# Two self-attention stages with their q·k products in float32 on 32-row head tiles instead of bfloat16 parts in one long stack

## The reference

```python
Q, K, V = (split_heads(x @ W.T) for W in (Wq, Wk, Wv))      # layer 0; 16 heads of 16
scores  = einsum('bhqd,bhkd->bhqk', Q, K) / 4 + mask        # mask: 0 where q-64 <= k <= q, else -1e9
x       = x + (softmax(scores) @ V merged) @ Wo.T           # on a normalised x

q, k, v = (split_heads(x @ W + b) for each of q, k, v)      # layer 1
x       = x + (softmax(q k^T / 4) @ v merged) @ Wo + bo     # all keys, no mask
```

## Time and profile before

| | us |
|---|---|
| median of three executions | 2630.13 |
| the profiled execution | 2628.91 |
| its span | 2627.2 |
| `l0at`: first projection to first exponential | 22.7 to 68.9 |
| `l0at`: first exponential to the last weigh | 68.9 to 272.4 |
| `l1at`: first projection to first exponential | 670.6 to 726.5 |
| `l1at`: first exponential to the last weigh | 726.5 to 981.5 |

### The profile page before, as it was taken

The page is one execution under the profiler, slowest core; times in us unless marked ns, Lnnn a source line. Parts: engine busy times, 40 slices in busy tenths (PEclk is TensorE's granted clock), DMA queues, the critical chain, the costliest instruction groups (busy, mean ns, idle before and its releaser), DMA issues. The chain is left out here.

```text
span 2627.2 us, 28469 instructions
## 1 busy us (share of the span) xinstructions
PE 2105.2 (80%) x10309; PEld 1316.8 (50%) x10309; DVE 1709.3 (65%) x2551; ACT 1191.6 (45%) x1889; POOL 587.0 (22%) x346
## 2 busy tenths in 40 slices
PE   5789889695599987969785888888798989283795
PEld 3456556584323324857641444444465654172574
DVE  5555355423677755731287999999864775957775
ACT  2334322110266663411056899999923235402340
POOL 2331112120241203012100566565200210000100
PEclk8899999698799998969987999999979989697896
DMA  6553120343655500034400000000021000000001
GB/s 125 90 87 44 62 97 1 106 151 120 106 73 73 65 1 22 1 109 158 138 33 32 1 1 1 1 1 1 34 91 37 0 1 0 0 8 5 17 1 39
DMA packets 107526, 126.70 MB, mean 48 GB/s; under 512 B 14823, under 2 KB 98676, under 8 KB 106357
## 3 DMA queue, kind: packets, MB, share of 16 engines
q1 hardware_dynamic: 99094, 112.27, 18.4%
q0 software_dynamic: 2880, 7.48, 0.8%
q10 hardware_dynamic: 5408, 5.07, 0.6%
HBM read 91.11 MB, written 33.29 MB: 47 GB/s over the span
## 5 line engine op out<-in xcount | busy, mean ns | idle before, releaser
L3351 DVE TENSOR_TENSOR_SCAN l2s_h<-l2w_aw 128x2048 f32<-128x2048 f32 x64 | 290.1, 4533 | 5.6 <-ACT l2s_rs L3474 5.6
L3279 PE MATMUL l2s_big<-g_xn,g_ident 128*128 128x512 f32 x512 | 259.5, 609 | 5.3 <-ACT l2s_dt L3478 4.2
L3438 POOL TENSOR_SCALAR l2w_aw<-l2w_aw 128x2048 f32<-128x2048 f32 x64 | 210.8, 3293 | 141.5 <-DVE l2w_aw L3343 136.3
L591 DVE TENSOR_REDUCE l1at_nm<-l1at_s 128x1 f32<-128x512 f32 x256 | 161.9, 683 | 64.0 <-PE l1at_s L441 63.1
L3271 PE MATMUL l2s_c_ps<-g_ident,l2s_h 128*128 128x128 f32 x1024 | 149.3, 279 | 55.5 <-ACT g_xn L3467 36.7
L3271 PEld LDWEIGHTS l2s_c_ps<-g_ident,l2s_h 128*128 128x128 f32 x1024 | 117.8, 142 | 146.2 <-issue 86.5
L691 ACT ACTIVATE g_xn<-l1at_s 128x512 f32<-128x512 f32 x256 | 143.6, 598 | 82.0 <-PE l1at_s L465 81.3
L3467 ACT ACTIVATE g_xn<-l2s_c_ps,l2s_ct 128x512 f32<-128x512 f32 x256 | 162.6, 685 | 16.2 <-PE l2s_c_ps L3271 15.9
L3460 ACT ACTIVATE l2w_aw<-l2s_dt,l2w_A 128x2048 f32<-128x2048 f32 x64 | 128.1, 2003 | 0.0
L591 DVE TENSOR_REDUCE l0at_nm<-l0at_s 128x2 f32<-128x384 f32 x128 | 69.7, 556 | 88.9 <-PE l0at_s L441 87.5
L3279 PEld LDWEIGHTS l2s_big<-g_xn,g_ident 128*128 128x128 f32 x512 | 82.3, 191 | 81.9 <-ACT g_xn L3467 59.0
(11 more groups left out here) (869 smaller groups left out, 4839.5 us busy)
## 6 DMA issues: line engine op xcount, KB each, us to landing
l1f_w<-in_L_ffn_w_dram SPq DMA_DIRECT2D x16, 1024.0 KB, 6.4
l0f_w<-L_ffn_experts_inter_dram SPq DMA_DIRECT2D x7, 1024.0 KB, 5.3
l0f_w<-n_L_ffn_experts_out_dram SPq DMA_DIRECT2D x7, 1024.0 KB, 9.8
l0at_qs<-l0at_parts SPq DMA_DIRECT2D x18, 256.0 KB, 8.7
l0at_ks<-l0at_parts SPq DMA_DIRECT2D x18, 256.0 KB, 18.0
l1at_qs<-l1at_parts SPq DMA_DIRECT2D x18, 256.0 KB, 8.8
l1at_ks<-l1at_parts SPq DMA_DIRECT2D x18, 256.0 KB, 20.5
expert_rows<-g_zeros SPq DMA_DIRECT2D x1, 4096.0 KB, 12.8
```

The costliest lines, as they stand in the source:

```text
L591: V.tensor_reduce(nm[:, s % 2, qts[0]:qts[-1] + 1, r], s1[:, u % 3, 0:len(qts) * KEYS].rearrange("p (q k) -> p q k", k=KEYS), AX, ALU.max, ...
L3279: nc.tensor.matmul(acc[:, tb, :], ident[:], hCT[:, tb, :], start=n == 0, stop=n == NST - 1).then_inc(acc_done, 1)
L3351: V.tensor_tensor_scan(out=h_all[:, i % 2].rearrange("p c t -> p (c t)"), data0=dA[:, i % 2].rearrange("p c t -> p (c t)"), data1=wd[:, i ...
L3438: nc.gpsimd.tensor_scalar(wd[:, i % 3], wd[:, i % 3], 10.0, -10.0, ALU.min, ALU.max).then_inc(clipped, 1)
```

## The change

Both calls use one new body:

- q and k stay float32 in SBUF (`qz`, `kz`). ACT writes each projection twice, once for the even and once for the odd heads (`e`), each with a per-row scale that is 0 in the other kind's rows. A head then has 32 rows, its 16 features and 16 rows of the other kind. The first of these is 1 in `kz` (a per-row bias, `top`) and holds the negated maximum in `qz`.
- Products of P (L460) and M (L439) use 32 rows, row tile `r`, in float32. Successive units take the row tiles 0, 1, 2, 3 in turn, M two tiles away from the P beside it.
- A group of a step is the 4 even or 4 odd heads of one half `o` of the features.
- Maxima go into padded columns `nmx`, are turned in float32 (L447) and added into `qz` by DVE (L596). The parts, their store and reload, L682 and POOL's L740 to L756 are gone; SP starts no DMA in the attention.
- `l0at`'s mask leaves PE. For M, DVE masks and reduces in one call per block (L587, two instructions each, four a unit). For P the exponentials of all 192 columns are taken and POOL then zeroes what the window excludes (`cut`, L726 and L728, per unit); `weigh` waits for it.
- M runs 14 (`l0at`) or 22 (`l1at`) units ahead instead of 16 or 32, and half of sequence 0's projections and its values lie between the first M units (EARLY). `weigh` comes every 4 units in both, 8 products each in `l0at`. `l0at`'s ring has 10 slots. The values' memset and the addition of `bo` move to POOL.

The core of the diff (removed bodies are in the listing above; "..." marks what is left out):

```diff
-    RING = 8
-    AT_NM, AT_TURN, AT_BACK, AT_Y, AT_LOAD = (1, 4, 6, 7, (3, 5)) if window else (3, 7, 11, 14, (8, 12))
+    NU = GH * QT // 2 if window else GH * QT
+    NW = NU // GH
...
+    RING = xn.shape[1] * DM // UNIT
+    LAG = 4 if window else 3
+    AT_MAX, AT_HEADS = (4, 6) if window else (12, 5)
+    AT_BACK, AT_OUT = ((1, 0), (1, 2)) if window else ((0, 7), (0, 9))
+    AT_QK, AT_V = (((0, 0, 1), (2, 0, 1)), (3, 0, 1)) if window else (((1, 8, 10), (2, 8, 10)), (3, 8, 10))
+    LEAD = 2 * NU + 2 - AT_MAX
+    EARLY = {3: ("qk", 1), 5: ("qk", KC + 1), 7: ("v", 0), 9: ("v", 1)}
...
+    def max_unit(m):
+        s, i = m // NU, m % NU
+        return s, (i + 2 - LEAD) % GH, ((2 * (i // GH), 2 * (i // GH) + 1) if window else (i // GH,))
...
-        qs, ks = (S.sb(n, [P, 2, HEADS, SEQ], BF16) for n in ("qs", "ks"))
+        qz, kz = (S.sb(n, [P, 2, KC, 2, SEQ]) for n in ("qz", "kz"))
...
+                def max_scores(m):
...
+                    if m >= 3:
+                        pe.wait_ge(s1_free, m - 2)
+                    rows = slice(HP * r, HP * (r + 1))
                     for v, q in enumerate(qts):
-                        k0 = max(q * P - 64, 0) if window else 0
-                        ins = nc.tensor.matmul(s1[:, u % 3, v * KEYS:(v + 1) * KEYS], qs[0:KROWS, b % 2, g * GH + r, q * P:(q + 1) * P],
-                                               ks[0:KROWS, b % 2, g * GH + r, k0:k0 + KEYS], start=not window, stop=not window or v == 1)
+                        k0, keys = (max(q * P - 64, 0), SPAN) if window else (0, SEQ)
+                        ins = nc.tensor.matmul(s1[:, m % 3, v * SPAN:v * SPAN + keys], qz[rows, b % 2, o, e, q * P:(q + 1) * P],
+                                               kz[rows, b % 2, o, e, k0:k0 + keys], start=True, stop=True)
                     ins.then_inc(s1_ready, 1)
...
                 def turn_maxima(s):
                     nm_at[s] = A.take(pe)
-                    pe.wait_ge(nm_made, s + 1)
-                    out = m_ps[KROWS:AROWS, 0, :].bitcast(BF16)
+                    pe.wait_ge(s1_free, (s + 1) * NU)
                     for q in range(QT):
-                        ins = nc.tensor.transpose(out[:, q * P:(q + 1) * P], nmp[:, s % 2, q].rearrange("p n r -> p (n r)"), identb[:])
+                        ins = nc.tensor.transpose(m_ps[:, 0, q * P:(q + 1) * P], nmx[:, s % 2, q, :], c["ident"][:])
...
+                def prob_scores(u):
+                    s, r, kts = prob_unit(u)
+                    b, o, e = place_of(s)
+                    if u % NU == 0:
+                        pe.wait_ge(A.free, nm_at[s])
                     if u >= 2:
                         pe.wait_ge(exp_done, u - 1)
...
+                        q0, n = columns(kt)
+                        ins = nc.tensor.matmul(s2[:, u % 2, v * SPAN:v * SPAN + n], kz[rows, b % 2, o, e, kt * P:(kt + 1) * P],
+                                               qz[rows, b % 2, o, e, q0:q0 + n], start=True, stop=True)
...
+                def weigh(w):
...
+                    pe.wait_ge(kept, (w + 1) * GH)
...
+                for u in range(-LEAD, TOTAL):
+                    s, i = u // NU, u % NU
+                    if u >= 0:
+                        prob_scores(u)
+                    if u + LEAD < TOTAL:
+                        max_scores(u + LEAD)
+                    if u + LEAD in EARLY:
+                        kind, n = EARLY[u + LEAD]
+                        project(0, n) if kind == "qk" else values(0, n)
+                    if u >= 0 and weighed_at(u) is not None:
+                        weigh(weighed_at(u))
+                    if i == AT_MAX and 0 <= s + 1 < NG:
+                        turn_maxima(s + 1)
+                    if s < 0:
...
+                def maximum(m):
...
+                    for v, q in enumerate(qts):
+                        to = nmx[:, s % 2, q, col:col + 1]
+                        if window:
+                            ins = V.tensor_tensor_reduce(masked[:, m % 3, v], s1[:, m % 3, v * SPAN:(v + 1) * SPAN], mask[:, 1 if q else 0, :], -1.0, 3e38,
+                                                         ALU.add, ALU.min, to)
+                        else:
+                            ins = V.tensor_reduce(to, s1[:, m % 3, :], AX, ALU.max, negate=True)
+                    ins.then_inc(s1_free, 1)
+
+                def place_maxima(s):
+                    b, o, e = place_of(s)
+                    dve.wait_ge(A.ready, nm_at[s])
+                    V.tensor_tensor(qz[:, b % 2, o, e, :], qz[:, b % 2, o, e, :], m_ps[:, 0, :], ALU.add).then_inc(A.free, 1)
...
                 def evacuate(b, j):
...
-                    E.activation(part[0][:, j, :], m_ps[:, at, :], ACT.Identity, bias=bias, scale=scale)
-                    E.activation(full[:, j, :], m_ps[:, at, :], ACT.Identity, bias=bias, scale=scale).then_inc(bank.free, 1)
...
+                    for e in range(2):
+                        if given:
+                            bias = qk_bias[:, n, o, e:e + 1]
+                        else:
+                            bias = top[:, 1 - e:2 - e] if n else 0.0
+                        ins = E.activation((qz, kz)[n][:, b % 2, o, e, :], m_ps[:, at, :], ACT.Identity, bias=bias, scale=own[:, n, e:e + 1])
+                    ins.then_inc(bank.free, 1)
...
+                def cut(u):
+                    pool.wait_ge(exp_done, u + 1)
+                    slot = pT[:, u % RING].rearrange("p (v t) -> p v t", t=SPAN)
+                    near, far = slot[:, :, 0:P], slot[:, :, SPAN - P:SPAN]
+                    Chain(pool, cut_step, u).step(G.affine_select(out=near, in_=near, compare_op=ALU.is_ge, fill=0.0, base=0, pattern=[[0, 2], [1, P]],
+                                                                  channel_multiplier=-1))
+                    G.affine_select(out=far, in_=far, compare_op=ALU.is_ge, fill=0.0, base=0, pattern=[[0, 2], [-1, P]],
+                                    channel_multiplier=1).then_inc(cut_done, 1)
```

More of the change, by code:

```diff
@@ L365, in self_attention @@
                 prepare(nc, name + "t", c, loads, jobs)
-        qs, ks = (S.sb(n, [P, 2, HEADS, SEQ], BF16) for n in ("qs", "ks"))
+        qz, kz = (S.sb(n, [P, 2, KC, 2, SEQ]) for n in ("qz", "kz"))
         vb = S.sb("vb", [P, 2, QT, HEADS, HP])
[L369 to L377, removed]
+        blocks, own, top = S.sb("blocks", [P, 2, 2 * GH]), S.sb("own", [P, 2, 2]), S.sb("top", [P, 2])
+        qk_bias = S.sb("qk_bias", [P, 2, KC, 2]) if given else None
+        mask = S.sb("mask", [P, 2, SPAN]) if window else None
+        masked = S.sb("masked", [P, 3, 2, SPAN]) if window else None
+        nmx = S.sb("nmx", [P, 2, QT, P])
         o_raw = S.sb("o_raw", [P, 2, SEQ])
@@ L555, in _ @@
-                for n in range(NG * QT - (LAG + WU - 1) // WU, NG * QT):
-                    weigh(n)
+                project(0, 0)
+                project(0, KC)
+                for u in range(-LEAD, TOTAL):
+                    s, i = u // NU, u % NU
+                    b, g = s // GROUPS, s % GROUPS
+                    if u >= 0:
[10 more added lines that the diff above has]
+                    if s < 0:
+                        continue
+                    if i == AT_HEADS and s:
+                        turn_heads(s - 1)
+                    if (g, i) == AT_BACK and b:
+                        turn_back(b - 1)
+                    if (g, i) == AT_OUT and b:
+                        outputs(b - 1)
+                    if b + 1 < BATCH:
+                        for o, (group, *steps) in enumerate(AT_QK):
+                            if g == group and i in steps:
+                                project(b + 1, steps.index(i) * KC + o)
+                        if g == AT_V[0] and i in AT_V[1:]:
+                            values(b + 1, AT_V[1:].index(i))
@@ L557, in _ @@
+                for w in range((TOTAL - LAG) // GH, TOTAL // GH):
+                    weigh(w)
                 turn_heads(NG - 1)
@@ L693, in copy_out @@
                 def copy_out(s):
[L694 removed]
+                    act.wait_ge(pv_done, (s + 1) * NW)
                     if s >= 2:
@@ new lines, in _ @@
+                ch = Chain(pool, built)
+                each, first = blocks[:, 0], blocks[:, 1]
+                ch.step(G.memset(each, 1.0))
+                ch.step(G.affine_select(out=each, in_=each, compare_op=ALU.is_ge, fill=0.0, base=0, pattern=[[-HD, 2 * GH]], channel_multiplier=1))
+                ch.step(G.affine_select(out=each, in_=each, compare_op=ALU.is_ge, fill=0.0, base=HD - 1, pattern=[[HD, 2 * GH]], channel_multiplier=-1))
+                ch.step(G.memset(first, 0.0))
+                ch.step(G.affine_select(out=first, in_=first, compare_op=ALU.not_equal, fill=1.0, base=0, pattern=[[-HD, 2 * GH]], channel_multiplier=1))
@@ L832 @@
+                if window:
+                    for u in range(TOTAL):
+                        cut(u)
 CTX, CD = 64, 192
```

419 lines of the change are left out of this document (120 added, 299 removed).

## The result

The changed kernel took 2685.11 us (median of 4, 2682.48 to 2685.32) against 2630.06: ratio 1.0203, 95% interval 1.0187 to 1.0220. Slower, as forecast, and inside the range, but by 55 us where 7 were forecast. That it is slower is clear of noise; whether by more than 2%, the interval leaves open. The profiled execution took 2684.89 us.

What follows compares the result with a forecast made beforehand. It took the leads as bound by the trip through memory and `l1at`'s main part by PE and ACT waiting for each other; 2628.9 - 24 - 25.5 - 27 + 80 + 3 = 2635.4, so about 2637 us, range 2598 to 2735.

Steps and rivals of the forecast that it cites:

- rival 1: P in both calls: passes of neighbouring products wait for each other, `l1at` round 5.2 us, total 2729; chance 0.13.
- The new P: P in float32 takes two passes; its result comes 1.13 us after its wait ends, against 0.39 in bfloat16.
- One round of `l1at` after: `l1at`: a chain of P, exponential and weigh, M hidden beside P, makes a round 4.43 us instead of 3.2 to 3.6.
- Main part of `l1at`, +83: `l1at` from its first exponential: 80 us longer by rounds, turns and once-per-sequence work, plus 3 for ACT's copies.
- The lead of `l1at`: `l1at` before its first exponential: 29.3 us instead of 55.9, -27, as the reload and PE's second step of M's go.
- Tails alike: Ends of both calls (turn, back, outputs): 13 us in both, no change.
- The main part of `l0at`: `l0at` after its lead: DVE's 8.6 us a step taken as the bound, 178 us instead of 203.5, -25.5.
- Rival 2: `l0at` bound by DVE or POOL at their upper prices: steps 1.7 us longer, +27, total 2665; chance 0.14.
- Rival 3: `l1at` rounds: the weigh needn't wait for P's end, a round 0.87 us shorter, -56, total 2581; chance 0.10.
- Rival 5: Clock falls to 1.2 GHz in the rounds because rows of 32 look idle, P's passes double: over 2750; chance 0.05.
- Rival 4: Both calls: all small choices (`l0at` step, friction, exponentials, leads) fall short, total 2611; chance 0.16.

Runs made afterwards that it cites:

- the two later ones: Changed kernel with POOL behind the columns, turning at 6 and M going on: 2653.99 us; new layer 0 with M going on, old layer 1: 2589.73 us.

## Why the prediction was right, and where not

- *The range*: the slowdown and its main cause, the round of `l1at`, were forecast by their mechanism. That 2685 lies inside is in part luck: the forecast's own range ended at 2662, and the range reached to 2735 for rival 1 (2729), which did not come true. What brought the time there, POOL beside DVE and the clock, had no term in the sum. The chance of slower was 0.55, little more than even.
- *"The new P"* and *"One round of `l1at` after"*: right, 4.34 against 4.43, and each part of the chain shows. The runs confirm its causes one by one: the second pass (bfloat16: 2.9), the two banks (three: 4.1 and 3.9, with M over 128 keys), M hidden (128 keys: 4.34).
- *Main part of `l1at`, +83*: 16 short. The step was 0.3 too long, 5 us too much; missing were the last step at half clock (27 us instead of 18.5: 8), four dips (6), a first step begun at a low clock (2.5) and 0.5 more for each pair of projections or values.
- *"The lead of `l1at`", -27*: this step failed. The sum has no term for the columns that ACT's first copy waits for, and I wrote that the values' memset on POOL costs nothing since POOL is idle. It and the addition of `bo` cost by what DVE did beside them: 15.6 us. Of the 21.6 missed, 6 are left; with POOL out of the way the lead still ran at a mean clock of 0.79. (The sum also counts one pair of M's too many, 1 us.) Moving the memset and the addition to the start of the block put them beside the only DVE work that the first M hangs on.
- *Tails alike*: +4.3 and +2.5. From the end of the last weigh to the last addition it is 11.8 and 12.6 us at 0.60 and 0.56, where before has 8.5 and 8.5 at 1.00. With M going on both are 8.5 again in that run; in the two later ones `l0at`'s is still 11.1 and 11.2, at 0.69 and 0.70.
- *"The main part of `l0at`"*: -21.9 against -25.5, by two errors that cancel. The bound is PE's 7.9 that I had worked out and set aside, not DVE's 8.6 (the read is hidden, 0.56 a unit). What comes once per sequence costs about 55 (181 less 16 x 7.9), not 40.
- *Rival 1* (passes wait for each other) is out: equal starts, 4.34; nor did the +17 us that I had estimated there come. (Its terms add up to 2727, not 2729.) *Rival 2* is out by the run without the selects and by bfloat16 in both layers. *Rival 3* (the weigh does not wait) is out: the gap from P6's start to the weigh is 1.06, the whole of both passes, and 0.32 where P has one. *Rival 5* had a chance of 0.05 and a price of over 110. The clock did fall, to a mean of 0.93 over the main part. I had argued against it from a stretch with full-height products, which says nothing on 32 rows. *Rival 4* needed a time under the forecast.

Open: what makes a dip fall behind one turning and not the next; the dips differ between executions of the same `l1at`, which was not tried further. Open too: why M over 128 keys ran at 0.77 with two banks for P and at 0.94 with three.
